# Four attention-and-FFN layers on one core: layer-3 keys made inside the adapter loop, layer-0 evictions ahead of the exponentials, straight attention programs

## The chip, the cores and the metric

One core of a Trainium2 chip. The metric is the device time of one execution in microseconds (us). The engines are named as in the profile: PE (TensorE, matmuls and transposes), PEld (its weight loads), DVE (VectorE), ACT (ScalarE), POOL (GpSimd) and SP (SyncE, which issues DMAs).

## What is computed

Sixteen sequences of 64 tokens with 512 channels go through four layers. Every layer adds an attention over a second input `ctx` and then a feed-forward part (FFN), both on a layer norm of x:

```python
x = x + _L2_xattn_ref(_layernorm(x), ctx_4096, mask, bias, Wq, Wk, Wv, Wo)      # layers 0, 2, 3: 32 heads of 128
x = x + _L2_ffn_ref(_layernorm(x), W_base, b_base, W_gate, W_thr, b_thr, A_w, B_w)
# FFN of layer 2:
w = w / wsum                                  # gate of 8 experts, thresholded
moe = jnp.einsum('ner,ne,eor->no', h, w, B_w) * SCALING
return base + moe.reshape(base.shape)
# attention of layer 3: 4 key/value heads, keys over context and latents
hidden_states = jnp.concatenate([context, latents], axis=1)
k = (hidden_states @ Wk); v = (hidden_states @ Wv)
```

## The kernel before

The program is a chain of blocks: setup, `a0` (attention of layer 0), `f0`, `x1`, `f1`, `a2`, `f2` (adapter FFN of layer 2), `a3`, `f3`. Tokens stand in eight tiles of 128. Every engine has its own in-order program, and semaphores tie them together. fp32 products are made as three fp16 matmuls of high and low halves (`mm3`, L85 to L87), so most values pass ACT (which writes the high half from PSUM) and DVE (which writes the rest as low half) before PE can use them. Weights come as slabs of 128x2048 that are turned to two fp16 halves the same way: a sum of squares on ACT (L434), the total on PE and DVE, a scale on POOL, the high half on ACT (L439) and the low half on DVE (L846).

**Attention.** `Attention.events(t)` lists the work of one period of 8 slots, the same list for all engines, each of which takes its own part of every event. A period covers one projection group; units of heads go through scores, turn, mix and out, one slot apart each. Periods 0 to 8 run in order; ACT, DVE, POOL and SP write periods 1 to 6 once as a hardware loop (`periods`, `Fori(0, 3)` over two periods), PE writes all of them out (`straight`). Period 8 has no projections: it drains the last units and does the first steps of the FFN that follows (`f_stat` statistics on DVE, `f_norm`, `f_turn` transposes on PE, `f_keep` ACT copies, `f_logit`, `f_main`).

In `a0` a query tile (128x512) is evicted by three ACT instructions, two for the squares of the norm (L536, L537) and the high half (L545), and two DVE ones (L947, L952); PE's `q_read` and the projection that follows wait for L952. ACT's list of a slot is: high half of the probabilities (`split_hi`, L579), slab squares (L434), four exponentials (L566), then the tile.

**f2 and layer 3's first steps.** `AdapterFFN` does per tile t: `base(t)` (L2125, four fp32 matmuls 128x512 into a PSUM bank; banks are reused every `deep` = 3 tiles, so base(t+3) waits for the x-add of tile t), a transpose of the gated tile `hw` (L2138), an ACT copy of it to `ht` (L1991), the adapter matmul `main(t)` (L2147) and the DVE x-add (L2094). Into the same loop are woven a3's slabs (`squares_ahead`, `total_ahead`, `high_ahead`, `low_ahead`), the halves of ctx (`ctx_high` L452, `ctx_low` L874), and the norm and transposes of x (`act_step`, `dve_step`, `pe_step`; PE's is L650). When all of it is done, 32 key and value tiles follow (`kv`), 12 matmuls each, alternating over two banks. SP issues the k and v slabs and ctx (2 MB) at the start of f2.

## Time and profile before

| | us |
|---|---|
| median of 3 runs | 2186.36 (2185.17 to 2188.26) |
| the profiled execution | 2187.63 |
| its span in the profile | 2185.8 |
| PE busy | 2057.9 (94% of the span) |
| DVE / ACT / POOL busy | 1343.3 / 1178.4 / 555.0 |
| mean granted TensorE clock | 0.977 |

The profile is taken from one execution. 1.8 us of that execution's time lie outside the span. PE is the busiest engine, so the views to read are those of PE's idle time and of the clock that it was granted. A row of the timeline gives start, length, engine, line, operation, output and input; a bracket behind it tells how long the engine was idle before and what ended that.

### The profile page before, as it was taken

To read this page: it belongs to the slowest core of one execution; us is meant where nothing else is said; L and a number is where in the kernel's file an instruction comes from. 1 tells how busy PE (TensorE), PEld (TensorE's weight loads), DVE (VectorE), ACT (ScalarE), POOL (GpSimd) and SP (SyncE) were. 2 spreads that over 40 slices of the span, in tenths; PEclk is the share of its full clock that TensorE was granted. 3 is DMA by queue.
4 is the path that set the end of the run, shared out by engine and by line. 5 is a ranking of instruction groups with operands and counts; after the bars stand their busy time and mean duration, and the time that the engine had idled before them with its cause. 6 is when DMAs were issued, how large, how long until landed. Compare 5 with 4: busy or idle time off the path is not lost.

```text
span 2185.8 us, 39604 instructions
## 1 busy us (share of the span) xinstructions
PE 2057.9 (94%) x13732; PEld 1131.0 (52%) x13732; DVE 1343.3 (61%) x2722; ACT 1178.4 (54%) x3031; POOL 555.0 (25%) x958
## 2 busy tenths in 40 slices
PE   6799999999879899999999999998889899999998
PEld 3566556656534345555555555555334455555564
DVE  6677776776763756656656656656542466666664
ACT  6677766766432455555555555533222576666651
POOL 4233233233241322122122122113200222222221
PEclk9899999999998999999999999999979999999999
DMA  3222122121002123232232232211200233333211
GB/s 131 61 67 62 45 66 60 47 81 35 27 10 119 61 78 76 71 92 76 71 92 76 72 92 76 51 35 44 113 20 1 63 78 78 82 78 82 59 49 39
DMA packets 181336, 142.92 MB, mean 65 GB/s; under 512 B 158139, under 2 KB 166587, under 8 KB 171283
## 3 DMA queue, kind: packets, MB, share of 16 engines
q1 hardware_dynamic: 180690, 140.37, 23.1%
q8 instruction: 110, 1.80, 0.3%
q14 instruction: 88, 0.71, 0.1%
q10 hardware_dynamic: 448, 0.03, 0.0%
HBM read 100.26 MB, written 2.10 MB: 47 GB/s over the span
## 4 chain that ended last, share of the span: by engine, by line
PE 66%; DVE 13%; ACT 11%; issue 6%; POOL 3%; DMA 0%; DVEq 0%; ACTq 0%; POOLq 0%; SPq 0%
PE bank L85 20%; PE bank L86 20%; PE bank L87 20%; ACT m_E L566 3%; PE bank L2125 3%; DVE m_Sm L1001 1%; ACT m_arena L545 1%; DVE m_x L1052 1%; ACT m_arena L434 1%; ACT m_arena L537 1%; DVE m_A L1046 1%; DVE m_nmax L1018 1%; ACT m_arena L536 1%; DVE m_arena L947 1%; DVE m_arena L846 1%
## 5 line engine op out<-in xcount | busy, mean ns | idle before, releaser
L947 DVE TENSOR_TENSOR m_arena<-bank,m_arena 128x512 f16<-128x512 f32 x320 | 221.1, 691 | 452.9 <-ACT m_arena L545 451.5
L85 PE MATMUL bank<-m_input_parts,m_arena 128*128 128x512 f16 x1120 | 431.0, 385 | 24.8 <-DVE m_arena L952 12.2
L86 PE MATMUL bank<-m_input_parts,m_arena 128*128 128x512 f16 x1120 | 430.2, 384 | 0.0
L87 PE MATMUL bank<-m_input_parts,m_arena 128*128 128x512 f16 x1120 | 429.9, 384 | 0.0
L1064 POOL TENSOR_TENSOR m_E<-m_E,m_rinv 128x512 f32<-128x512 f32 (+1 forms) x192 | 172.2, 897 | 815.0 <-DVE m_rinv L1032 815.0
L566 ACT ACTIVATE m_E<-m_Sm,m_nmax 128x64 f32<-128x64 f32 (+1 forms) x512 | 185.2, 362 | 254.3 <-DVE m_nmax L1022 149.0
L545 ACT ACTIVATE m_arena<-bank 128x512 f16<-128x512 f32 x320 | 189.1, 591 | 232.5 <-PE bank L87 232.3
L85 PE MATMUL bank<-m_wo_t,m_A 128*128 128x512 f16 x768 | 292.4, 381 | 0.0
L86 PE MATMUL bank<-m_wo_t,m_A 128*128 128x512 f16 x768 | 292.2, 381 | 0.0
L87 PE MATMUL bank<-m_wo_t,m_A 128*128 128x512 f16 x768 | 292.0, 380 | 0.0
L1052 DVE SCALAR_TENSOR_TENSOR m_x<-bank,m_osc,m_x 128x512 f32<-128x512 f32 x192 | 143.2, 746 | 79.1 <-PE bank L87 75.5
L85 PE MATMUL bank<-m_arena,m_input_parts 128*128 128x128 f16 (+1 forms) x768 | 186.6, 274 | 2.4 <-DVE m_arena L952 1.6
L85 PEld LDWEIGHTS bank<-m_input_parts,m_arena 128*128 128x128 f16 x1120 | 110.4, 99 | 151.2 <-DVE m_arena L952 14.3
L86 PE MATMUL bank<-m_arena,m_input_parts 128*128 128x128 f16 (+1 forms) x768 | 186.7, 274 | 0.0
L87 PE MATMUL bank<-m_arena,m_input_parts 128*128 128x128 f16 (+1 forms) x768 | 186.7, 274 | 0.0
L87 PEld LDWEIGHTS bank<-m_input_parts,m_arena 128*128 128x128 f16 x1120 | 110.4, 99 | 136.4 <-issue 7.0
L86 PEld LDWEIGHTS bank<-m_input_parts,m_arena 128*128 128x128 f16 x1120 | 110.5, 99 | 116.7 <-issue 6.2
L579 ACT ACTIVATE m_split<-m_E 128x512 f16<-128x512 f32 (+1 forms) x174 | 97.1, 558 | 121.6 <-POOL m_E L1064 117.3
L1061 POOL TENSOR_TENSOR m_w_scale<-m_w_tot,m_consts 128x1 f32<-128x1 f32 x84 | 46.6, 554 | 454.6 <-DVE m_w_tot L840 435.7
L562 ACT ACTIVATE m_E<-bank,m_nmax,m_qk 128x128 f32<-128x128 f32 x256 | 113.5, 452 | 67.4 <-DVE m_nmax L989 67.4
L1046 DVE TENSOR_TENSOR m_A<-bank,m_A 128x512 f16<-128x512 f32 x192 | 130.2, 678 | 6.0 <-ACT m_A L585 5.1
L846 DVE SCALAR_TENSOR_TENSOR m_arena<-m_raw,m_w_scale,m_arena 128x2048 f16<-128x2048 f32 (+1 forms) x58 | 118.0, 2034 | 15.4 <-ACT m_arena L439 13.5
(308 smaller groups left out, 4154.5 us busy)
## 6 DMA issues: line engine op xcount, KB each, us to landing
m_raw<-a_q SPq DMA_DIRECT2D x24, 1024.0 KB, 5.0
m_raw<-a_o SPq DMA_DIRECT2D x24, 1024.0 KB, 5.0
m_raw<-a_k SPq DMA_DIRECT2D x9, 1024.0 KB, 4.9
m_raw<-a_v SPq DMA_DIRECT2D x9, 1024.0 KB, 5.3
m_bias_in<-bias SPq DMA_DIRECT2D x64, 128.0 KB, 2.1
m_arena<-f_w SPq DMA_DIRECT2D x3, 1024.0 KB, 7.6
...
```

The costliest lines, as they stand in the source:

```text
L85: pe.matmul(out, lhs[0], rhs[0], start=first, stop=False)
L86: pe.matmul(out, lhs[0], rhs[1], start=False, stop=False)
L87: return pe.matmul(out, lhs[1], rhs[0], start=False, stop=last)
L545: act.activation(self.dest(name, part, 0), self.shaped(name, src), ACT.Copy).then_inc(s["proj_hi"].sem, 1)
L562: ins = act.activation(k.E[:, b % 2, cols], bank[2 + b % 2][:, cols], ACT.Exp, bias=k.nmax2[:, b % 2, h:h + 1], scale=qk, accum_out=k.rsum ...
L566: ins = act.activation(k.E[:, b % 2, cols], k.Sm[:, b % 2, cols], ACT.Exp, bias=k.nmax[:, b % 2, h:h + 1], accum_out=k.rsum[:, b % 2, h:h ...
L579: act.activation(self.split_dst(b, 0), k.E[:, b % 2, 0:self.keys * HG], ACT.Copy)\
L846: dve.scalar_tensor_tensor(out=self.slab(kind, par, 1), in0=self.raw(j, kind), scalar=self.k.w_scale[:, j % 2:j % 2 + 1], in1=self.slab(ki ...
L947: ins = dve.tensor_tensor(self.dest(name, part, 1), self.shaped(name, bank[m % 2][:, :]), self.dest(name, part, 0), ALU.subtract)
L1046: dve.tensor_tensor(self.mix_dst(b, 1), self.mix_src(), self.mix_dst(b, 0), ALU.subtract).then_inc(s["mixed_lo"].sem, 1)
L1052: dve.scalar_tensor_tensor(out=k.x[:, pair, :], in0=bank[6][:, :], scalar=k.osc[:, g:g + 1], in1=k.x[:, pair, :], op0=ALU.mult, op1=ALU.ad ...
L1064: pool.tensor_tensor(out, a, b, op).then_inc(sem.sem, 1)
```

## The change

- **a0, slots 0 and 4 of periods 1 to 7** (`pair`): ACT does the slab squares ahead of the high half of the probabilities, and the first query tile's three evictions ahead of the four exponentials. PE and DVE keep the tile where it was.
- **Straight programs**: ACT, DVE and POOL write all nine periods of all three attentions out; SP keeps its loop.
- **Layer 3's preparation begins in a2's last period**: SP loads both slabs in period 7, ctx in two halves in period 8; the joint scale, all of ctx's halves and the first slab (keys) are converted between the steps of period 8. `ctx_in` lies in the arena, and the turned tiles of f2 in other free pieces.
- **The adapter loop of f2 and f3**: the eight transposes of `hw` go to two banks, four each, and two 128x512 ACT copies take them back into `hw`. Main(t) is followed by base(t+3). In f2, steps 4 to 11 make two of the 16 key tiles each, in banks 5 and 6; the 16 value tiles stay behind the loop.

```diff
+            pair = self.layer == 0 and slot in (0, 4) and not opening
+            sooner = squared is not None and (pair or self.layer == 3)
+            if sooner and pair:
+                out.append(("w_squares", squared))
             if self.by_dma(t, b - 1):
                 out.append(("split_hi", b - 1))
+            if sooner and not pair:
+                out.append(("w_squares", squared))
+            if pair and todo:
+                out.append(("act_tile", todo[0], slot // 4))
...
-                out.append(("tile", todo.pop(0), slot // 4))
+                out.append(("tile_act_sooner" if pair else "tile", todo.pop(0), slot // 4))
...
+            if t == 8 and self.layer == 2:
+                out += {0: [("n_joint",)], 2: [("n_ctx", 0)], 3: [("n_ctx", 1), ("n_squares",)], 4: [("n_sum",), ("n_ctx", 2)],
+                        5: [("n_ctx", 3)], 6: [("n_convert",)]}.get(slot, [])
...
+    def load_slabs(self, sp):
+        for j in range(2):
+            self.load(sp, self.pre[j], 0, j, 0)
+    def load_ctx(self, sp, c):
+        sp.dma_start(self.k.ctx_in[:, c:c + 2, :], self.dram["ctx_t"][:, c:c + 2, :]).then_inc(self.s["ctx_in"].sem, 16)
...
+                    if t == 7 and slot == 4:
+                        self.next.follower.load_slabs(sp)
+                    elif t == 8 and slot in (0, 2):
+                        sp.wait_ge(*(s["mixed"] if slot else s["scores"]).by(UNITS - 4))
+                        self.next.follower.load_ctx(sp, slot)
...
-        if self.layer == 3 and 3 <= t < 3 + KC:
-            self.ctx_high(act, t - 3)
...
+    def kv_tile(self, n):
+        return (n % 4) * 4 + n // 4 if n < 16 else n
+    def kv_bank(self, n):
+        return self.k.bank[5 + n % 2 if n < 16 else n % 2][:, :]
...
+    def kv_pe(self, pe, n):
+        k, s = self.k, self.s
+        if n == 0:
+            pe.wait_ge(*s["w_lo"].by(1))
+            pe.wait_ge(*s["ctx_lo"].by(KC))
+        if n < 16 and n % 4 == 0:
+            pe.wait_ge(*s["xt_lo"].by(n // 2 + 2))
+        pe.wait_ge(*s["kv_lo"].by(n - 1))
...
+    def keys_of(self, t):
+        return range(2 * (t - 4), 2 * (t - 4) + 2) if 4 <= t < 12 else []
...
-            for m in range(32):
-                act.wait_ge(*s["kv"].by(m + 1))
-                act.activation(k.kv3(m, 0), bank[m % 2][:, :], ACT.Copy).then_inc(s["kv_hi"].sem, 1)
+            for n in range(16, 32):
+                self.kv_act(act, n)
...
-        self.periods(act, emit)
+        self.straight(emit)
...
-        self.periods(dve, emit, ch, self.CHAIN["dve"][self.layer])
+        self.straight(emit)
...
-        self.periods(pool, emit, self.own, self.CHAIN["pool"][self.layer])
+        self.straight(emit)
...
-        for t in range(TILES):
-            if self.follower and t % 2 == 0 and t // 2 < self.follower.NP:
-                self.follower.squares_ahead(act, t // 2)
-            act.wait_ge(*s["ht"].by(t + 1))
-            act.wait_ge(*s["main"].by(t - 1))
-            act.activation(self.ht[:, t % 2, :], self.turn_bank(t), ACT.Copy).then_inc(s["ht_s"].sem, 1)
-            if self.follower and t % 2 and t // 2 < self.follower.NP:
-                self.follower.high_ahead(act, t // 2)
-            if self.follower:
-                self.follower.act_step(act, t)
-        for t in range(TILES, TILES + 2):
-            if self.follower:
-                self.follower.act_step(act, t)
+        for h in range(2):
+            act.wait_ge(*s["ht"].by(h + 1))
+            act.activation(self.hw[:, 4 * h:4 * h + 4, :].rearrange("p t n -> p (t n)"), self.turn_bank(h), ACT.Copy)\
+               .then_inc(s["ht_s"].sem, 1)
+        if self.follower:
+            for t in range(TILES + 5):
+                for n in self.follower.keys_of(t - 1):
+                    self.follower.kv_act(act, n)
+                if t // 2 + 1 < self.follower.NP:
+                    (self.follower.high_ahead if t % 2 else self.follower.squares_ahead)(act, t // 2 + 1)
+                if t < TILES + 2:
+                    self.follower.act_step(act, t)
...
-            if self.follower and t // 2 < self.follower.NP:
-                if t % 2 == 0:
-                    self.follower.total_ahead(dve, t // 2)
-                else:
-                    self.follower.low_ahead(dve, t // 2)
             if self.follower:
-                self.follower.dve_step(dve, t)
-        for t in range(TILES, TILES + 2):
+                self.ahead_dve(dve, t)
             if self.follower:
-                self.follower.dve_step(dve, t)
+                for n in self.follower.keys_of(t):
+                    self.follower.kv_dve(dve, n)
+        if self.follower:
+            for t in range(TILES, TILES + 5):
+                self.ahead_dve(dve, t)
+                for n in self.follower.keys_of(t):
+                    self.follower.kv_dve(dve, n)
+    def ahead_dve(self, dve, t):
+        if t // 2 + 1 < self.follower.NP:
+            (self.follower.low_ahead if t % 2 else self.follower.total_ahead)(dve, t // 2 + 1)
+        if t < TILES + 2:
+            self.follower.dve_step(dve, t)
...
-        turn(0)
-        turn(1)
+        for h in range(2):
+            for t in range(4 * h, 4 * h + 4):
+                pe.wait_ge(*s["hw"].by(t + 1))
+                ins = pe.transpose(self.turn_bank(h)[:, (t % 4) * P:(t % 4 + 1) * P], self.hw[:, t, :], k.ident[:, :])
+            ins.then_inc(s["ht"].sem, 1)
         for t in range(TILES):
-            pe.wait_ge(*s["ht_s"].by(t + 1))
-            pe.matmul(self.main_bank(t), self.ht[:, t % 2, :], self.bm[:, :], start=False, stop=True).then_inc(s["main"].sem, 1)
-            if self.follower and t % 2 == 0 and t // 2 < self.follower.NP:
-                self.follower.sum_ahead(pe, t // 2)
-            if t + 2 < TILES:
-                turn(t + 2)
+            pe.wait_ge(*s["ht_s"].by(t // 4 + 1))
+            pe.matmul(self.main_bank(t), self.hw[:, t, :], self.bm[:, :], start=False, stop=True).then_inc(s["main"].sem, 1)
             if t + self.deep < TILES:
                 self.base(pe, t + self.deep)
             if self.follower:
-                self.follower.pe_step(pe, t)
-        for t in range(TILES, TILES + 2):
-            if self.follower:
-                self.follower.pe_step(pe, t)
+                self.ahead_pe(pe, t)
+        if self.follower:
+            for t in range(TILES, TILES + 4):
+                self.ahead_pe(pe, t)
+    def ahead_pe(self, pe, t):
+        if t % 2 == 0 and t // 2 + 1 < self.follower.NP:
...
+            self.follower.sum_ahead(pe, t // 2 + 1)
+        if t < TILES + 2:
+            self.follower.pe_step(pe, t)
+        for n in self.follower.keys_of(t):
+            self.follower.kv_pe(pe, n)
```

The first place is ACT in a0, slot 4 of a period; what stands there before (`m_split` is the high half of the probabilities, L534/L553 register work):

```order
L585 ACTIVATE m_A<-bank 128x2x4x64 [waits outp,mixed]
L579 ACTIVATE m_split<-m_E 128x256 [waits pt1,probs]
L434 ACTIVATE m_arena,m_w_ss<-m_raw 128x2048 [waits raw1,proj]
L553 REGISTER_ALU
L566 ACTIVATE m_E,m_rsum<-m_Sm,m_nmax 128x64 [waits split_lo,top]
L566 ACTIVATE m_E,m_rsum<-m_Sm,m_nmax 128x64 x3
L533 REGISTER_ALU [waits scores]
L534 REGISTER_ALU [waits a0_q_tot]
L536 ACTIVATE m_arena<-bank 128x8x64 [waits proj]
L537 ACTIVATE m_arena<-bank 128x8x64
L545 ACTIVATE m_arena<-bank 128x8x64 [waits proj]
```

And now, in the changed program (L482 is L434 of before, L668 is L579, L625/L626/L634 are L536/L537/L545, L655 is L566):

```order
L674 ACTIVATE m_A<-bank 128x2x4x64 [waits outp,mixed]
L482 ACTIVATE m_arena,m_w_ss<-m_raw 128x2048 [waits raw1,proj]
L668 ACTIVATE m_split<-m_E 128x256 [waits pt1,probs]
L625 ACTIVATE m_arena<-bank 128x8x64 [waits proj,a0_q_tot,scores]
L626 ACTIVATE m_arena<-bank 128x8x64
L634 ACTIVATE m_arena<-bank 128x8x64 [waits proj]
L655 ACTIVATE m_E,m_rsum<-m_Sm,m_nmax 128x64 [waits split_lo,top]
L655 ACTIVATE m_E,m_rsum<-m_Sm,m_nmax 128x64 x3
```

The squares moved ahead of the wait for the probabilities, and the tile ahead of the exponentials. The second place is DVE at the end of slot 2 of a2's last period; before:

```order
L1046 TENSOR_TENSOR m_A<-bank,m_A 128x512 [waits mixed_hi]
L1052 SCALAR_TENSOR_TENSOR m_x<-bank,m_osc,m_x 128x512 [waits outp]
L1213 BN_STATS m_bn<-m_x 128x6 [waits xadd]
L1215 BN_AGGR m_mv<-m_bn 128x2 [waits f2_dve]
L1217 TENSOR_SCALAR m_var<-m_mv 128x1 [waits f2_dve]
L1011 SCALAR_TENSOR_TENSOR m_Sm<-bank,m_qk,m_bias_in 64x4x64 [waits a2_bias_sum,exped,scores]
```

Now (L1130 is L1052 of before, L953 is `ctx_low`, L1293 is L1213, L1089 is L1011):

```order
L1124 TENSOR_TENSOR m_A<-bank,m_A 128x512 [waits mixed_hi]
L1130 SCALAR_TENSOR_TENSOR m_x<-bank,m_osc,m_x 128x512 [waits outp]
L953 SCALAR_TENSOR_TENSOR m_input_parts<-m_arena,m_joint,m_input_parts 128x16x64 [waits a3_ctx_hi]
L1293 BN_STATS m_bn<-m_x 128x6 [waits xadd]
L1295 BN_AGGR m_mv<-m_bn 128x2 [waits f2_dve]
L1297 TENSOR_SCALAR m_var<-m_mv 128x1 [waits f2_dve]
L1089 SCALAR_TENSOR_TENSOR m_Sm<-bank,m_qk,m_bias_in 64x4x64 [waits a2_bias_sum,exped,scores]
```

A low half of ctx stands between x and its statistics; the same in slots 3, 4 and 5. The third place is PE in the adapter loop, from main(4) on; before:

```order
L2147 MATMUL bank<-m_arena 128x512 [waits f2_ht_s]
L639 MATMUL bank<-m_w_ss,m_ones_b 128x1 [waits w_ss,misc_read]
L2138 MATMUL bank<-m_ident,m_arena 128x128 [waits f2_ht_s,f2_hw]
L2125 MATMUL bank<-m_arena 128x512 [waits x,xt_s]
L2125 MATMUL bank<-m_arena 128x512 x3
L650 MATMUL bank<-m_ident,m_Sm 128x128 [waits xt_lo,xn]
L650 MATMUL bank<-m_ident,m_Sm 128x128 x3
L2147 MATMUL bank<-m_arena 128x512 [waits f2_ht_s]
```

Now (L2243 is L2147, L2221 is L2125, L739 is L650, and L85 to L87 are the first matmuls of key tile 0):

```order
L2243 MATMUL bank<-m_arena 128x512 [waits f2_ht_s]
L2221 MATMUL bank<-m_arena 128x512 [waits x,xt_s]
L2221 MATMUL bank<-m_arena 128x512 x3
L739 MATMUL bank<-m_ident,m_Sm 128x128 [waits xt_lo,xn]
L739 MATMUL bank<-m_ident,m_Sm 128x128 x3
L85 MATMUL bank<-m_input_parts,m_arena 128x512 [waits xt_lo,a3_kv_lo,a3_ctx_lo,w_lo]
L86 MATMUL bank<-m_input_parts,m_arena 128x512
L87 MATMUL bank<-m_input_parts,m_arena 128x512
```

The transpose of `hw` is gone from the loop, and the key matmuls stand in it.

## Rows read from the trace of the kernel before

**Rows 1.** Busy time by stage: stretch, length, busy per engine, granted clock, DMA share, GB/s.
```profile
100.00:500.00 400.00, 389.69 (x3697) 243.18 (x3696) 283.62 (x679) 286.92 (x858) 137.24 (x241) 1.00 0.22 59
800.00:1480.00 680.00, 678.87 (x4198) 349.74 (x4196) 415.56 (x756) 353.18 (x842) 144.80 (x259) 1.00 0.28 74
1485.00:1546.42 61.42, 51.62 (x340) 35.12 (x338) 37.11 (x75) 18.79 (x59) 22.15 (x27) 0.92 0.27 104
...
1552.19:1697.80 145.61, 126.06 (x481) 56.36 (x482) 56.76 (x94) 39.59 (x59) 12.30 (x32) 0.88 0.06 22
1610.73:1697.80 87.07, 85.66 (x384) 38.02 (x385) 22.12 (x32) 19.88 (x33) 0.00 (x0) 0.97 0.00 1
1736.00:2100.00 364.00, 364.00 (x2365) 201.78 (x2363) 230.64 (x419) 243.02 (x655) 84.49 (x147) 1.00 0.31 75
```

**Rows 2.** Waits of 90 to 560 us: us in total, times, longest us.
```profile
PE bank L85 <- DVE m_arena L952: 10.7, 13, 2.1
...
DVE m_Sm L1001 <- issue: 2.6, 2, 1.7
```

**Rows 3.** Timeline of ACT in a0, one slot of these thirteen.
```profile
318.58 0.42 ACT L579 ACTIVATE m_split<-m_E 128x256 f16<-128x256 f32 x1 [1.74 <-POOL m_E L1064]
318.91 1.89 ACT L434 ACTIVATE m_arena<-m_raw 128x2048 bf16<-128x2048 f32 x1
...
322.12 0.57 ACT L536 ACTIVATE m_arena<-bank 128x512 f32<-128x512 f32 x1
```

**Rows 4.** Timeline of PE, the wait of that slot and the longest of the thirteen.
```profile
325.04 0.39 PE L85 MATMUL bank<-m_input_parts,m_arena 128*128 128x512 f16 x1 [0.97 <-DVE m_arena L952]
...
358.71 0.39 PE L85 MATMUL bank<-m_input_parts,m_arena 128*128 128x512 f16 x1 [2.12 <-DVE m_arena L952]
```

**Rows 5.** Busy time by stage, two stretches with a low clock.
```profile
359.00:364.00 5.00, 5.00 (x17) 1.89 (x16) 3.96 (x11) 2.06 (x11) 1.28 (x4) 0.66 0.00 2
...
1591.50:1616.00 24.50, 16.12 (x40) 7.46 (x41) 16.59 (x26) 7.46 (x12) 2.98 (x6) 0.51 0.13 44
```

**Rows 6.** Timeline of DVE in a2's last period.
```profile
1508.64 0.55 DVE L1223 TENSOR_SCALAR m_arena<-m_x,m_mv,m_rstd 128x512 f32<-128x512 f32 x1
...
1512.91 0.69 DVE L1213 BATCH_NORM_STATS2 m_bn<-m_x 128x6 f32<-128x512 f32 x1
...
1515.46 0.98 DVE L1011 SCALAR_TENSOR_TENSOR m_Sm<-bank,m_qk,m_bias_in 64x256 f32<-64x256 f32 x2 [1.45 <-POOL m_bias_in L1064]
...
1523.30 1.48 DVE L1223 TENSOR_SCALAR m_arena<-m_x,m_mv,m_rstd 128x512 f32<-128x512 f32 x1 [0.66 <-POOL m_rstd L1244]
```

**Rows 7.** Timeline of POOL beside the last of these.
```profile
1523.23 1.26 POOL L1318 TENSOR_TENSOR m_x<-m_x,m_arena 128x512 f32<-128x512 f32 x1
```

**Rows 8.** Groups of instructions of 1485 to 1611 us: busy, mean ns.
```profile
L874 DVE SCALAR_TENSOR_TENSOR m_input_parts<-m_arena,m_joint,m_input_parts 128x1024 f16<-128x1024 f32 x4 | 5.1, 1274 | 0.0
...
L846 DVE SCALAR_TENSOR_TENSOR m_arena<-m_raw,m_w_scale,m_arena 128x2048 f16<-128x2048 f32 x2 | 4.7, 2344 | 0.0
```

**Rows 9.** Timeline of PE in the adapter loop.
```profile
1563.09 1.02 PE L2147 MATMUL bank<-m_arena 128*128 128x512 f32 x2
1563.95 0.17 PE L639 MATMUL bank<-m_w_ss,m_ones_b 128*128 128x1 bf16 x1
...
1564.98 3.67 PE L2125 MATMUL bank<-m_arena 128*128 128x512 f32 x8 [0.70 <-DVE m_x L2094]
1568.49 0.60 PE L650 MATMUL bank<-m_ident,m_Sm 128*128 128x128 f32 x4
...
1579.83 2.07 PE L2147 MATMUL bank<-m_arena 128*128 128x512 f32 x2 [3.78 <-ACT m_arena L1991]
```

**Rows 10.** Waits of 1552 to 1611 us.
```profile
PE bank L2147 <- ACT m_arena L1991: 10.3, 5, 3.8
```

**Rows 11.** Timeline of DVE at the start of f2: the gated tiles.
```profile
1551.12 1.70 DVE L2088 TENSOR_TENSOR m_arena<-m_arena 128x128 f32<-128x128 f32 x8
```

**Rows 12.** Waits of the whole program, with no releaser in the profile.
```profile
DVE m_Sm L1011 <- issue: 5.0, 2, 2.6
```

131 lines of the change are left out of this document (85 added, 46 removed).

## The prediction

> **What bounds the kernel now.** I read the busy time by stage first. PE is busy for 364.00 of 364.00 us in the middle of layer 3's attention and for 678.87 of 680 in layer 2's [rows 1]: there the time is the count of matmuls, and no edit of another engine's program can shorten it. PE stands still in three other places. In a0 it is busy 389.69 of 400 us. In a2's last period it is busy 51.62 of 61.42 us. From the first adapter matmul to the end of the value tiles it is busy 126.06 of 145.61 us, at a granted clock of 0.88 [rows 1]. The change touches these three and leaves PE's work as it is, but for some transposes. So each part is worth the idle time, and the half-clock time, that it takes from PE there.
>
> The profiled execution took 2187.63 us, and the median is 1.27 below it. The sum is made against 2187.63, and the 1.27 come off at the end.
>
> **a0.** The waits name what PE stood for: 10.7 us in 13 gaps at its projection matmul, for DVE's L952 [rows 2]. One slot shows the chain. ACT sits idle 1.74 us for the probabilities, then does their high half, 1.89 us of slab squares from 318.91, the exponentials, and only at 322.12 the first of the tile's three evictions [rows 3]; PE gets its operand at 325.04 after 0.97 us of idling, and in the worst slot after 2.12 [rows 4]. The squares need only a slab that lies there, so ahead of the wait they take its 1.74 us. The tile goes ahead of exponentials that last from 320.80 (318.91 + 1.89) to 322.12, 1.3 us. The tile is then ready about 3 us sooner, more than the longest gap. What comes later for it? The exponentials, by the tile's 322.12 to about 323.6, 1.5 us, less the 1.7 that the squares no longer cost them: nothing net. The next thing queued behind them, the high half of the next probabilities, waits for POOL anyway. One of the 13 gaps (0.26) is in the opening period, which the change leaves alone, so 10.7 − 0.3 = **−10.4**. One more thing hangs on the longest gap: right behind it PE ran at a mean clock of 0.66 over 5 us [rows 5], about 3.4 us at the lower level of 1.2 GHz, which costs half of that, **−1.7**. Sum −12.1. Bounds: if half of the gaps close and another wait shows up in the others, −5; with all of it and the smaller waits beside it, −14. I take the upper part, as the margin of 3 us stands against gaps of 0.25 to 2.12.
>
> **Straight programs.** Their price is more code; their gain is that the jump at a loop's end goes. Such jumps show as DVE waits with no releaser: 2.6 us in two in a0 [rows 2], 5.0 in two in a2 [rows 12]. PE has no idle time in a2, so there they are covered and worth **0**; in a0 they lie inside the gaps just counted. If the cover is gone they cost 1.7 to 2.6 us each. That the longer programs stall for their own fetch is a rival below.
>
> The Trainium skill (Runtime: NRT & Kernel Launch, Instruction fetch mechanics) says that a taken branch to a page that isn't loaded stalls, while straight code is fetched ahead and mostly hidden. The waits of [rows 2, 12] agree with its first half; by its second half the straight programs cost nothing, which is what the sum has; were it wrong for programs of this length, the fetch rival below would be the case.
>
> **a2's last period.** Here work is added, some 5.1 us of ctx's low halves and 2.35 of a slab's low half on DVE [rows 8], and the like on ACT and POOL. ACT mostly waits in this period, so its part hides, except where it delays a copy that PE wants. DVE's part stands between x and its statistics. In slot 2 it is on the path: statistics at 1512.91 lead over POOL's rstd and the mask bias to the scores at 1515.46 [rows 6], so a low half of 1.27 us comes on top in full: +1.3. In slots 3 to 5 PE's own 12 out-matmuls of some 2.6 us (at the 0.216 worked out below) cover a part of each; I take 0.6 of 1.27 for each, +1.9 in all. In slot 6 the slab's low half of 2.35 stands ahead of the last tile's statistics; there some 0.3 are slack: +2.1. Sum **+5.3**. Bounds: 0, if everything hides, and 4 × 1.27 + 2.35 + 1 for ACT's part = +8.5. All added DMAs (two slabs and ctx, 4 MB) are issued 10 us or more ahead of their first reader, on an SP queue that has nothing else urgent, and read by engines that wait until then anyway: 0. If ctx came late, its first reader would hold up all of DVE in slot 2.
>
> On this place a rule of the Trainium skill bears. The row: a norm of 128x512 takes 0.55 us alone but 1.48 when POOL's L1318 runs beside it [rows 6, 7]. The Trainium skill (SBUF — State Buffer, SBUF: two separate sides) says that VectorE and GpSimd share one port pair as an exclusive lock, so that one of them blocks for the other's whole instruction. The low halves read two tiles from SBUF and would meet L1318 in slots 2 and 3; by the rule that is 0.3 each, +5.9 in place of +5.3. The sum goes without it.
>
> **The adapter loop.** First its start. Before, main(0) could go when the first transpose had been copied. Now all eight transposes stand ahead of it, so it waits for the last gated tile, which DVE ends at 1551.12 + 1.70 = 1552.82 [rows 11]. Main(0) then comes at about 1553.15 in place of 1552.19: **+1.0**.
>
> Then the loop to the end of the values, 145.61 us before, with the 1.42 at its end that stay [rows 1]. What PE has to do at full clock: eight mains of 0.86 (1563.09 to 1563.95), five bases of 3.51 (1564.98 to 1568.49) and eight turns of 0.44 (three quarters of the 0.60 of their row are seen apart, the rest overlaps) [rows 9], and 32 tiles of 12 matmuls. The latter took 85.66 us for 384 [rows 1]; the first 5.3 us of it are the end of the half-clock stretch [rows 5], in which 12 are done, so one is (85.66 − 5.3) / 372 = 0.216. Sum 6.9 + 17.6 + 3.5 + 0.3 for small ones + 384 × 0.216 = 82.9, in all 111.2. What remains to wait: five bases each wait for the x-add of the main before them. Before, 0.70 us were seen behind a transpose of 0.3 [rows 9], so now some 1.1 each, 5.7 in all; and 1.8 more where DVE is busy with a slab's low half (2.35) in steps 1 and 3. Together 118.7. From step 4 on each step has two key tiles, 5.2 us of PE work, and DVE's and ACT's share of a step is about 4.3 us or less, so PE is the bound: the 10.3 us that main waited for ACT's small copies [rows 10], with 3.78 the longest [rows 9], are gone, and with them, I expect, the half clock: over 24.5 us from 1591.5 it was 0.51 [rows 5], in a stretch in which PE was busy 16.12 us only. 145.61 − 1.42 = 144.2, so **−25.5**. Bounds: −14 if the clock stays low as it did, −27 if the added waits vanish.
>
> **f3** has the same new start (+0.65) and saves about 0.11 on three bases: **+0.3**. **Clock**: longer idle stretches in a2's last period, whose clock is 0.92 already [rows 1], can bring another fall of 3.4 us; I count one, **+1.7** (0 to +3.4).
>
> **Sum**: −12.1 + 5.3 + 1.0 − 25.5 + 0.3 + 1.7 = −29.3, so 2158.3 for the profiled execution and **2157** for the median. Chance 0.55 for this case, by which I mean 2153 to 2162.
>
> **Rivals.**
> - *The clock stays halved in the loop.* PE fell to 1.2 GHz at 1592 and stayed there for some 24 us [rows 5]. If the idling of the first steps (waits of 1.1 to 2 us each) brings such a stretch, the key tiles run at half speed for 20 us and lose 10: **2167**. For it: it happened in this very loop. Against: from 1552 to 1563 PE idled as much, and the two falls in it came after longer waits. Chance 0.16.
> - *a0's gain goes elsewhere.* The tile is early, but PE then waits in another slot for scores or probabilities, now pushed by the tile on ACT. Then a0 gives 5 in place of 12: **2164**. For it: the exponentials' readers are a chain over POOL. Against: they end no later than before. Chance 0.12.
> - *The tail costs little.* If the added conversions hide (ACT is idle for most of the period) and no new fall comes, 5 to 6 us less: **2151**. Chance 0.11.
> - *Slower: instruction fetch.* The straight programs of ACT and DVE are some 40% longer in instructions. Were they to stall as at the loops' ends, 1.7 us each [rows 2], PE would have to see more than 29 / 1.7 = 17 such stalls before the gain is gone; with 20 of them, **2192**. Against it: PE's program is straight already, is by far the longest, and shows 364.00 of 364.00 us busy [rows 1]. Chance 0.04.
> - *It doesn't do what it says.* If the key tiles stay blocked until the loop's end (through the two banks that the transposes of `hw` also use, or a late low half of ctx), PE idles as before there and only half of the 25 is won: **2169**. Chance 0.02.
>
> **Range.** 2147 to 2168 leaves out some 2 in 10: a part of the first and the last rivals, and what lies below. A measurement of this kernel can tell about 0.2%, 4.4 us. Faster by more than that 0.94, within it 0.02, slower 0.04; all but the fetch rival lie far below 2182.
>
> **What the next profile would show.** a0: the wait of PE for L952's successor falls from 10.7 to under 1, PE busy in over 398 of 400 us, no stretch at a clock of 0.66. Last period of a2: PE's idle time grows from 9.8 to some 15 us, spread over slots 2 to 7, with DVE named. Loop: 119 us or so from main(0) to the last value matmul, clock near 1.0, and waits for x-adds of 1 to 2 us in the first five steps alone. I would be wrong if ACT turned up as what PE waits for in steps 4 to 11, if a long half-clock stretch lay there, or if waits with no releaser stood all over ACT's and DVE's rows.

## The result

The changed kernel takes 2151.10 us (median of 3 runs, 2149.67 to 2152.86) where the kernel before takes 2186.36. The ratio is 0.9838 (95% interval 0.9816 to 0.9860): 35 us, or 1.6%, faster. The forecast was 2157, with a range of 2147 to 2168. It held, and the kernel is 6 us faster than the likeliest case. Run again beside other kernels, it took 2152.88 (2149.55 to 2153.63), ratio 0.9836. One execution of a kernel below, the one with the late low halves, took 2690.0 us at a granted clock of 0.75, and it is left out of that kernel's numbers.

The page of its profiled execution (2149.67 us) begins:

```profile
span 2147.9 us, 38029 instructions
...
PE 2040.1 (95%) x13732; PEld 1125.9 (52%) x13732; DVE 1336.4 (62%) x2722; ACT 1175.9 (55%) x3019; POOL 557.6 (26%) x958
```

PE has as many matmul records as before and is busy 17.8 us less. A fall of the busy time is no fall of the work. Where 1.2 GHz is granted, the same matmul is busy for twice as long (in the kernel before, the records of the base matmuls, L2125, follow one another after 0.85 us at 1586 us and after 0.43 at 1566), and the last matmul before a pause is shown as busy for longer than it holds up a stream (below).

To compare stages I cut both programs at records that both have: DVE's adds into x. Counting those of the three attentions, the 1st and the 57th bound the stretch called a0 below, its seven full periods; the 65th is the first of a2; the 121st is the first of a2's last period; the first add of f2 starts the adapter loop; the 129th is the first of a3. The stretch from the 121st to f2's first is called the tail. Busy time by stage in the changed kernel (stretch, length, busy of PE, PEld, DVE, ACT, POOL, granted clock, DMA share, GB/s):

```profile
88.77:532.11 443.34, 441.40 (x4245) 277.61 (x4242) 322.75 (x782) 325.26 (x976) 153.11 (x261) 1.00 0.21 58
532.11:807.04 274.93, 241.70 (x1197) 122.30 (x1196) 167.01 (x340) 111.05 (x230) 82.00 (x116) 0.95 0.17 60
1463.31:1541.14 77.83, 61.71 (x367) 38.51 (x365) 49.67 (x106) 28.73 (x72) 24.50 (x31) 0.91 0.20 68
1541.14:1698.00 156.86, 141.37 (x650) 65.99 (x651) 66.35 (x113) 52.82 (x97) 20.31 (x46) 0.99 0.09 26
```

| stage | before | changed | difference | forecast |
|---|---|---|---|---|
| start to a0's first x-add | 89.09 | 88.77 | -0.3 | 0 |
| a0 | 460.16 | 443.34 | -16.8 | -12.1 |
| a0's last period, f0, x1, f1, a2's start ("the stage behind a0") | 277.63 | 274.93 | -2.7 | 0 |
| a2, seven periods | 656.26 | 656.26 | 0 | 0 |
| the tail: a2's last period to f2's first x-add | 70.22 | 77.83 | +7.6 | +5.3 +1.0 +1.7 |
| f2's loop and the values, to a3's 129th x-add | 182.93 | 156.86 | -26.1 | -25.5 |
| from there through f3, to the last x-add | 446.39 | 446.71 | +0.3 | +0.3 |

So the forecast stands in five stages within 0.6 us, and misses in two: a0, by 4.7, and the stage behind a0, which the change touches by the straight programs alone, by 2.7. The waits of PE in a0 answer to [rows 2]. Of the thirteen behind L952 (now L1030) none is left:

```profile
PE bank L85 <- DVE m_arena L1041: 1.0, 1, 1.0
PE bank L85 <- issue: 0.8, 1, 0.8
```

ACT in one slot of the new order, which answers to [rows 3]. The tile's first eviction starts 2.69 us behind the start of L674; before, it started 5.87 us behind the start of the same instruction (L585 at 316.25, L536 at 322.12), so it comes 3.2 us sooner:

```profile
308.92 0.60 ACT L674 ACTIVATE m_A<-bank 128x512 f16<-128x512 f32 x1
309.42 1.90 ACT L482 ACTIVATE m_arena<-m_raw 128x2048 bf16<-128x2048 f32 x1
...
311.31 0.40 ACT L668 ACTIVATE m_split<-m_E 128x256 f16<-128x256 f32 x1
311.61 0.58 ACT L625 ACTIVATE m_arena<-bank 128x512 f32<-128x512 f32 x1
...
313.17 0.35 ACT L655 ACTIVATE m_E<-m_Sm,m_nmax 128x64 f32<-128x64 f32 x1
```

From 100 to 500 us PE is now busy 399.03 of 400 us, where 389.69 were read before [rows 1] and over 398 were forecast.

PE in the adapter loop, which answers to [rows 9]. L2243 is main, L2221 base, L739 a turn:

```profile
1540.51 0.59 PE L2243 MATMUL bank<-m_arena 128*128 128x512 f32 x1
1541.98 3.67 PE L2221 MATMUL bank<-m_arena,m_wo_t 128*128 128x512 f32 x8 [0.87 <-DVE m_x L2184]
1545.48 0.17 PE L728 MATMUL bank<-m_w_ss,m_ones_b 128*128 128x1 bf16 x1
1545.51 1.10 PE L2243 MATMUL bank<-m_arena 128*128 128x512 f32 x2
```

And its waits up to 1610 us, which answer to [rows 10]:

```profile
PE bank L2221 <- DVE m_x L2184: 6.1, 5, 1.7
```

The 10.3 us for ACT's small copies are gone. What stands in their place is what was foreseen, five waits for x-adds, 6.1 us where 7.5 were assumed. From main(0) to the last value matmul:

```profile
1539.98:1658.11 118.13, 112.04 (x475) 51.35 (x474) 47.94 (x83) 31.45 (x46) 12.80 (x28) 1.00 0.05 18
```

118.13 us were measured where 118.7 were forecast, and 112.04 of PE work where 111.2 were.

### The profile page after: what moved, and what is told of

Its sections match the earlier page's. It is cut to its first block, busy times and chain, and to the rows that moved or that the text cites. A ratio compares the mean times of both kernels' runs of the same rounds, so it can differ in the third digit from the quotient of the medians.

```text
span 2147.9 us, 38029 instructions
## 1 busy us (share of the span) xinstructions
PE 2040.1 (95%) x13732; PEld 1125.9 (52%) x13732; DVE 1336.4 (62%) x2722; ACT 1175.9 (55%) x3019; POOL 557.6 (26%) x958
## 4 chain that ended last, share of the span: by engine, by line
PE 81%; DVE 9%; ACT 5%; issue 3%; POOL 1%; DMA 0%; ACTq 0%; SPq 0%; DVEq 0%; POOLq 0%
PE bank L85 25%; PE bank L86 25%; PE bank L87 25%; PE bank L2221 2%; ACT m_E L655 1%; DVE m_bn L1293 1%; PE bank L1981 1%; ACT m_E L651 1%; DVE m_x L1130 1%; ACT m_arena L487 1%; DVE m_arena L925 1%; DVE m_wo_t L925 1%; PE bank L2243 1%; DMA m_raw<-a_q 0%; PE bank L825 0%
## 5 line engine op out<-in xcount | busy, mean ns | idle before, releaser
L85 PE MATMUL bank<-m_input_parts,m_arena 128*128 128x512 f16 x1120 | 428.4, 383 | 12.6 <-ACT m_input_parts L1779 3.7
L87 PE MATMUL bank<-m_input_parts,m_arena 128*128 128x512 f16 x1120 | 427.6, 382 | 0.0
L634 ACT ACTIVATE m_arena<-bank 128x512 f16<-128x512 f32 x320 | 189.3, 592 | 238.6 <-PE bank L87 238.2
L655 ACT ACTIVATE m_E<-m_Sm,m_nmax 128x64 f32<-128x64 f32 (+1 forms) x512 | 185.4, 364 | 240.2 <-DVE m_nmax L1100 148.5
L85 PE MATMUL bank<-m_wo_t,m_A 128*128 128x512 f16 x768 | 292.6, 381 | 0.0
L87 PE MATMUL bank<-m_wo_t,m_A 128*128 128x512 f16 x768 | 292.4, 381 | 0.0
L1130 DVE SCALAR_TENSOR_TENSOR m_x<-bank,m_osc,m_x 128x512 f32<-128x512 f32 x192 | 143.2, 746 | 78.9 <-PE bank L87 76.7
L85 PE MATMUL bank<-m_arena,m_input_parts 128*128 128x128 f16 (+1 forms) x768 | 186.6, 274 | 2.4 <-DVE m_arena L1030 1.6
L87 PE MATMUL bank<-m_arena,m_input_parts 128*128 128x128 f16 (+1 forms) x768 | 186.7, 274 | 0.0
L87 PEld LDWEIGHTS bank<-m_input_parts,m_arena 128*128 128x128 f16 x1120 | 110.3, 98 | 134.7 <-issue 4.7
L85 PEld LDWEIGHTS bank<-m_input_parts,m_arena 128*128 128x128 f16 x1120 | 110.2, 98 | 133.4 <-issue 5.8
L1139 POOL TENSOR_TENSOR m_w_scale<-m_w_tot,m_consts 128x1 f32<-128x1 f32 x84 | 47.6, 566 | 459.4 <-DVE m_w_tot L919 441.3
L668 ACT ACTIVATE m_split<-m_E 128x512 f16<-128x512 f32 (+1 forms) x174 | 97.0, 558 | 85.2 <-POOL m_E L1142 85.2
L925 DVE SCALAR_TENSOR_TENSOR m_arena<-m_raw,m_w_scale,m_arena 128x2048 f16<-128x2048 f32 (+1 forms) x58 | 117.4, 2024 | 13.8 <-ACT m_arena L487 13.1
```

The costliest lines, as they stand in the source:

```text
L85: pe.matmul(out, lhs[0], rhs[0], start=first, stop=False)
L87: return pe.matmul(out, lhs[1], rhs[0], start=False, stop=last)
L634: act.activation(self.dest(name, part, 0), self.shaped(name, src), ACT.Copy).then_inc(s["proj_hi"].sem, 1)
L655: ins = act.activation(k.E[:, b % 2, cols], k.Sm[:, b % 2, cols], ACT.Exp, bias=k.nmax[:, b % 2, h:h + 1], accum_out=k.rsum[:, b % 2, h:h ...
L668: act.activation(self.split_dst(b, 0), k.E[:, b % 2, 0:self.keys * HG], ACT.Copy)\
L925: dve.scalar_tensor_tensor(out=self.slab(kind, par, 1), in0=self.raw(j, kind), scalar=self.k.w_scale[:, j % 2:j % 2 + 1], in1=self.slab(ki ...
```

## Experiments

Each kernel is the changed one, or the one before, with the edit that is shown.

### a0: the order undone, and the order alone

```diff
-            pair = self.layer == 0 and slot in (0, 4) and not opening
-            sooner = squared is not None and (pair or self.layer == 3)
+            pair = False
+            sooner = squared is not None and ((self.layer == 0 and slot in (0, 4) and not opening) or self.layer == 3)
```

> The changed kernel with a0's ACT order as before (squares behind the probabilities' high half, tile behind the exponentials); all else stays. Theory 1: a0 gave 16.8 us between the first and the 57th x-add, because each of the 13 gaps cost PE more than the idle that the row shows (some 0.2 us each: the last matmul before a gap is shown with 0.38 us, while in a stream the next follows after 0.216), and because the straight programs took the two loop-end stalls. Then undoing the order alone gives back 16.8 less what the loop ends had: 0.75 + 1.57 us of gap and the 1.7 us of half clock behind the longest, so +12.8: about 2164. Rival: what exceeds the predicted 12.1 comes from the straight programs alone; then the order is worth 10.4 less 2.3 = 8.1, about 2159. In the trace: gaps of 0.54 and 0.97 us at PE's projection matmul, and neither 1.30 nor 2.12.

Measured: 2167.86 us (2167.34 to 2168.34), ratio to before 0.9914 (0.9896 to 0.9932). Its a0:

```profile
90.22:546.47 456.25, 444.02 (x4245) 277.77 (x4242) 326.18 (x782) 325.37 (x975) 154.26 (x261) 1.00 0.21 57
```

a0 takes 12.9 us longer than in the changed kernel, where +12.8 was expected. Between the two profiled executions the whole is 18.2 us longer; of the other 5.3, 1.5 lie in the start and 3.6 in the stage behind a0, which vary from run to run (below). Against before, which had the loops, a0 is 3.9 shorter: that is what straight programs give by themselves, the two long gaps and the half clock behind one of them (expected: 0.75 + 1.57 + 1.7 = 4.0).

The other way round, the kernel before with the new order in a0 and its hardware loops kept:

> The kernel before with a0's new ACT order alone, hardware loops kept. Theory 1 (the order alone closes all gaps, the loop-end stalls of 1.7 us lie inside the 3 us by which the tile is early, and each gap cost 0.2 more than its idle): -16.8, about 2169.6. Rival (the straight programs are needed for the two loop-end gaps and the half clock behind one): -12.8, about 2173.6, with PE gaps at the loop ends.

Measured: 2171.80 us (2165.12 to 2172.80), ratio 0.9924 (0.9900 to 0.9947). Its a0:

```profile
89.55:532.89 443.34, 441.40 (x4245) 277.64 (x4242) 322.96 (x781) 325.41 (x976) 152.91 (x261) 1.00 0.22 58
```

443.34 us, the same to the hundredth as with straight programs. The order alone brings all 16.8. The median lies halfway between the two expected values, since the other stages differ by 1 to 3 us from run to run; the stage decides. Theory 1 stands: the two edits overlap, and the lead of the tile covers the loops' ends.

### The hardware loops kept

```diff
-        self.straight(emit)
+        self.periods(act, emit)
```

and so for DVE and POOL.

> The changed kernel with the hardware loops of ACT, DVE and POOL as before; all else stays. Theory 1 (the loop ends stall DVE and ACT 1 to 2.6 us, but the tile is some 3 us early in a0 and PE is covered in a2 and a3): no change that can be told, 2151 within 3 us, with waits without a releaser back in DVE's and ACT's rows and no PE gap behind them. Rival (the straight programs are what made a0 gain more than forecast): 2 to 5 us slower, with PE gaps at the two loop ends near 220 and 345 us.

Measured: 2153.95 us (2153.39 to 2154.87), ratio 0.9852 (0.9834 to 0.9869), against 0.9838 and 0.9836 for the changed kernel: no difference that can be told. The stalls at the loops' ends are back in the waits of the whole program, in a2 where PE has no idle time:

```profile
DVE m_Sm L1089 <- issue: 5.0, 2, 2.5
ACT m_split L668 <- issue: 4.4, 2, 2.3
```

a0 takes 443.35 us. In the changed kernel these two rows are absent; of waits without a releaser, one of 0.2 us on DVE in a0 is left, none in a2 and none on ACT. So the fetch rival is out as well: the straight programs, some 50% (ACT) and 30% (DVE) longer in instructions, stall no more, and they bring nothing either, once the order in a0 is as it is.

### a0: only the squares, only the tile

```diff
-            if pair and todo:
-                out.append(("act_tile", todo[0], slot // 4))
```

with `("tile", ...)` in its old place for all engines.

> The changed kernel, but in a0 only the slab squares go ahead of the probabilities' high half; the tile stays behind the exponentials. Theory 1 (the gaps close by whatever lead the tile gets): the squares fill ACT's 1.7 us of idling, so exponentials and tile come some 1.9 sooner, more than the gaps of 0.54 and 0.97 that straight programs leave; a0's stage from the first to the 57th x-add stays at 443.3 us. Rival (the tile must stand ahead of the exponentials, since what follows them pushes back): some of the 12.9 us that a0 loses without the new order come back, 447 us or more.

Measured: 2159.91 us in one run. Its a0:

```profile
88.79:541.38 452.59, 443.80 (x4245) 277.76 (x4241) 325.95 (x781) 325.36 (x976) 154.26 (x261) 1.00 0.21 57
```

The expectation failed: 9.3 of the 12.9 us come back. ACT's timeline says why:

```profile
313.25 1.90 ACT L480 ACTIVATE m_arena<-m_raw 128x2048 bf16<-128x2048 f32 x1
...
315.14 0.41 ACT L666 ACTIVATE m_split<-m_E 128x256 f16<-128x256 f32 x1
317.00 0.35 ACT L653 ACTIVATE m_E<-m_Sm,m_nmax 128x64 f32<-128x64 f32 x1 [1.45 <-DVE m_nmax L1094]
...
318.34 0.57 ACT L623 ACTIVATE m_arena<-bank 128x512 f32<-128x512 f32 x1
```

The squares went into the 1.74 us of idling, and a new idle time of 1.45 opened ahead of the exponentials, which wait for DVE's maximum. The tile behind them came 0.3 us sooner, and the gaps of 0.97 and 0.56 became 0.68 and 0.26. On this run theory 2 was formed. With only the tile moved (squares behind it):

> The changed kernel, but in a0 only the tile goes ahead of the exponentials; the squares stay behind the probabilities' high half, now behind the tile. Theory 2 (formed on the run with the squares alone, whose gaps fell by 0.28 us only: the exponentials wait for DVE's maximum, so squares moved ahead of them bring the tile little; it is the tile's own move into that time that counts): PE's gaps at the tile stay away and a0's stage is 443.3 us, as with both moves, unless the exponentials, which now start 1.9 us later behind the squares, come back as gaps elsewhere, up to 14 x 0.5 us = 7. Rival (both moves are needed): 447 to 452 us.

Measured: 2164.65 us in one run. Its a0, and PE's waits in it:

```profile
89.69:546.16 456.47, 446.11 (x4244) 276.00 (x4241) 328.84 (x781) 322.50 (x975) 154.34 (x261) 1.00 0.21 57
```
```profile
PE bank L85 <- DVE m_arena L1028: 5.1, 11, 0.5
PE bank L85 <- DVE m_arena L1039: 1.8, 1, 1.8
PE bank L726 <- ACT m_arena L480: 1.2, 1, 1.2
```

456.47 us: nothing is gained over 456.25 with neither. The squares, 1.9 us long, now stand between the tile and the exponentials, everything behind them comes later, and other tiles are late by 0.46. So theory 2 falls too. The stage lies above both what the theory (443.3, at most 7 more) and what the rival (447 to 452) allowed. Neither move is worth much by itself (3.7 and -0.2 us, each from one run's stage); together they are worth 12.9. The squares fill the wait for the probabilities, the tile fills the wait for the maximum that this opens.

### The key tiles behind the loop

```diff
-        return range(2 * (t - 4), 2 * (t - 4) + 2) if 4 <= t < 12 else []
+        return []
...
-            for n in range(16, 32):
+            for n in range(32):
```

> The changed kernel with no key tile in the adapter loop: all 32 tiles follow it, in the same order and banks. Theory 1 (the gain of the loop is key work put where PE waited for the x chain of DVE and ACT): from step 4 on PE has 1.3 us per step against some 3.7 of DVE, six such steps leave some 14 us idle, and the clock falls for a time as before (+3 to +10): 2168 to 2176. Rival (the gain is that of the two transposed banks, since before, PE waited 10.3 us for the small ACT copies): +3 to +5, 2154 to 2156.

Measured: 2164.21 us (2160.89 to 2166.37), ratio 0.9900 (0.9883 to 0.9918): 13.1 us slower than the changed kernel, 11.3 beside its repeat. Between the two theories. The stage, and PE in the loop's last steps:

```profile
1541.46:1709.15 167.69, 147.03 (x649) 67.24 (x650) 66.66 (x113) 53.05 (x97) 20.32 (x46) 0.95 0.08 24
```
```profile
1574.41 0.66 PE L739 MATMUL bank<-m_ident,m_Sm 128*128 128x128 f32 x4 [1.46 <-DVE m_Sm L938]
...
1577.21 0.66 PE L739 MATMUL bank<-m_ident,m_Sm 128*128 128x128 f32 x4 [1.28 <-DVE m_Sm L938]
1580.02 2.37 PE L739 MATMUL bank<-m_ident,m_Sm 128*128 128x128 f32 x8 [2.15 <-DVE m_Sm L938]
```

The stage is 10.8 us longer. Without keys PE idles 5.2 us more (4.9 of it in three waits for DVE's norm) and has 5.7 us more of busy time for the same work, at a clock of 0.95 in place of 0.99. I had expected 14 us of idling. From the last base (1566.68) to the first key matmul (1583.80) PE had 17.1 us, less than the 22 that six steps of 3.7 us would take: the last x-adds of DVE start at 1572.07, 1574.87 and 1577.67, so its step is 2.8 us and not 3.7.

### The two banks alone

In the kernel before, the transposes go to two banks and two copies take them back; nothing else is changed.

```diff
-            act.activation(self.ht[:, t % 2, :], self.turn_bank(t), ACT.Copy).then_inc(s["ht_s"].sem, 1)
...
+        for h in range(2):
+            act.wait_ge(*s["ht"].by(h + 1))
+            act.activation(self.hw[:, 4 * h:4 * h + 4, :].rearrange("p t n -> p (t n)"), self.turn_bank(h), ACT.Copy)\
+               .then_inc(s["ht_s"].sem, 1)
```

> The kernel before, with the eight transposes of the gated tile in two banks and two ACT copies back into it ahead of the loop, and nothing else changed. Theory 1 (in the loop before, PE waited 10.3 us for small ACT copies that stood behind slab and ctx work in ACT's queue, and the clock fell behind the longest of these waits): they go, the start comes 1.0 later, some of the idling moves to the turns; -8 to -14, 2172 to 2178. Rival (without key tiles PE waits for the turns instead, as long as before): within 3 us of 2186.

Measured: 2182.88 us (2177.16 to 2186.18), ratio 0.9984 (0.9972 to 0.9997), 3 us. That is at the edge of what the rival allowed and far from the 8 to 14 us of the theory: the rival is right. PE's waits in the loop, to be read against [rows 10]:

```profile
PE bank L650 <- DVE m_Sm L859: 10.5, 4, 5.3
...
PE bank L639 <- ACT m_arena L434: 4.5, 2, 2.8
PE bank L2126 <- DVE m_x L2095: 3.0, 3, 1.2
```

The 10.3 us behind ACT's copies did not go, they moved: to the turns behind DVE's norm and to the slab sums behind ACT's squares. The stage takes 178.39 us. With it the 26 us of the loop can be laid out, in the one order in which the parts were added: 182.93 before, 178.39 with the banks (-4.5), 167.69 when slab and ctx work have moved to a2's last period too (-10.7, for which that period pays 7.6 less the later start), 156.86 with the keys in the loop (-10.8). The move to a2's last period was not run without the banks.

### a2's last period: where the added work goes

First, the next tile's statistics ahead of the added low halves:

```diff
-            if t == 8 and self.layer == 2:
-                out += {0: [("n_joint",)], 2: [("n_ctx", 0)], 3: [("n_ctx", 1), ("n_squares",)], ...
             if t == 8 and slot < 7:
                 out.append(("f_stat", slot + 1))
+            if t == 8 and self.layer == 2:
+                out += {0: [("n_joint",)], 2: [("n_ctx", 0)], 3: [("n_ctx", 1), ("n_squares",)], ...
```

> The changed kernel, but in a2's last period DVE does the statistics of the next tile ahead of ctx's and the slab's low half, and so on all engines in that place. Theory 1 (the low halves stood on the path x-add, statistics, rstd, bias, scores): slot 2 gives back 1.4 us, which now lie in DVE's 1.45 us wait for the bias, slot 3 and slots 4 to 6 about 0.6 each; -3.4, about 2147.7. Rival (PE or ACT set the pace of this period, the low halves ride along): within 1 us of 2151.

Measured: 2155.22 us (2154.36 to 2155.72), ratio 0.9863 (0.9846 to 0.9879). The tail takes 78.4 us, as in the changed kernel (77.8; 78.3 in its repeat). The gain failed to come, and not for the rival's reason. DVE, then POOL, in slot 2:

```profile
1498.15 0.15 DVE L1297 TENSOR_SCALAR m_var<-m_mv 128x1 f32<-128x1 f32 x1
1498.22 1.27 DVE L953 SCALAR_TENSOR_TENSOR m_input_parts<-m_arena,m_joint,m_input_parts 128x1024 f16<-128x1024 f32 x1
1500.73 0.98 DVE L1089 SCALAR_TENSOR_TENSOR m_Sm<-bank,m_qk,m_bias_in 64x256 f32<-64x256 f32 x2 [1.23 <-POOL m_bias_in L1142]
```
```profile
1498.38 1.52 POOL L1328 TENSOR_TENSOR m_rstd<-m_var,m_consts 128x1 f32<-128x1 f32 x1 [0.90 <-DVE m_var L1297]
1499.88 0.72 POOL L1142 TENSOR_TENSOR m_bias_in<-m_bias_in,m_mask 128x256 f32<-128x256 f32 x1
```

DVE started the low half in its idle time, but the POOL instruction that this idle time waits for, 128x1 elements, took 1.52 us beside it in place of 0.55. Of the 1.27 us that were to be hidden 0.97 came back as POOL's. It is no chance of one slot. Five of POOL's eight rstd instructions began beside a low half in this run; they took 1.52, 1.52, 1.58, 1.52 and 2.61 us, and each ended 0.41 us behind DVE's instruction, the last one beside the slab's low half of 2.35:

```profile
1527.73 2.35 DVE L925 SCALAR_TENSOR_TENSOR m_arena<-m_raw,m_w_scale,m_arena 128x2048 f16<-128x2048 f32 x1
```
```profile
1527.88 2.61 POOL L1328 TENSOR_TENSOR m_rstd<-m_var,m_consts 128x1 f32<-128x1 f32 x1 [2.15 <-DVE m_var L1297]
```

The other three took 0.55. In the changed kernel low half and rstd stood apart, and all eight took 0.55; another 128x1 instruction of POOL, the slab's scale (L1139 at 1512.14), stood beside the third low half there and took 1.52.

So in the second version only two low halves stay in the slots, and the rest goes where DVE waits for the last logits:

```diff
+            if t == 8 and self.layer == 2:
+                out += {2: [("n_low", 0)], 3: [("n_low", 1)], 7: [("n_low", 2), ("n_low", 3), ("n_wlow",)]}.get(slot, [])
```

with ACT's high halves in their slots and its squares in slot 2.

> The changed kernel, but in a2's last period only two low halves of ctx stay (each behind the statistics of its slot); the other two and the slab's low half go to the end of slot 7, where DVE waits 5.5 us for the last logits (they take 4.9), and the slab's squares go to slot 2, where ACT waits 5.6 us. Theory 1: the tail loses all but some 1 us of the 6.7 that it grew by, -5.5, about 2145.6, with the same loop behind it. Rival (the conversions are not what lengthened the tail, or they push the gates in their new place): within 2 us of 2151. The clock's falls in the tail can shift either by 2 to 3 us.

Measured: 2147.61 us, the median of three (2143.36 to 2149.18), ratio 0.9817 (0.9795 to 0.9840). The tail takes 71.69 us, 6.1 less than in the changed kernel, about as expected. By the medians the whole gained 3.5 us, and the intervals overlap; the two profiled executions differ by 0.5 only, since the start was 1.6, the stage behind a0 2.9 and the loop 0.9 longer this time. In the third version the squares and one high half of ctx go to the start of slots 2 and 3 and one low half behind the norm of slot 3:

> The changed kernel, with every added conversion of a2's last period put into an idle stretch that its trace shows: the slab's squares at the start of slot 2 and the second high half of ctx at the start of slot 3 (ACT waits 5.4 us there for the maximum), its low half behind the norm in slot 3 (DVE waits 1.25), the first low half behind the statistics, two low halves and the slab's at the end of slot 7 (5.5 us). Theory: the tail from the last looped x-add to f2's first takes 70.5 us or so, as before the change (70.2), against 71.7 with only the lows late and 77.8 in the changed kernel; in all 5 to 7 us faster than the changed kernel run beside it, if the clock falls alike. Rival (ACT's high halves in slots 4 to 6 or the late lows still lengthen it): 72 us or more.

Measured: 2145.40 us (2143.36 to 2149.03), ratio 0.9807 (0.9793 to 0.9821), beside the changed kernel itself on the same chip with 2152.88, ratio 0.9836 (0.9823 to 0.9850): 7.5 us faster, and the intervals don't meet. The tail:

```profile
1466.36:1538.58 72.22, 60.56 (x367) 39.91 (x365) 50.83 (x106) 28.96 (x72) 25.49 (x31) 0.93 0.21 74
```

72.22 us, where 70.5 was expected and 72 or more was the rival's mark, so by the tail the rival is right, though the whole gained 7.5 where the theory said 5 to 7. I had left out two things of my own: f2's start, 0.9 us later by its transposes, and POOL's 0.97 in slot 2, since one low half still stands beside its rstd. By the tail alone this version is no better than the second (71.69); of the 7.3 us between its profile and that of the changed kernel's repeat, 6.1 lie in the tail, 1.3 in the stage behind a0 and 1.3 in the loop, less 1.5 for a longer start. The late low halves are not free either: in both versions they meet POOL's 128x512 instruction into x (L1413, L1417), and one of them takes 2.3 us in place of 1.27, POOL's 2.2 in place of 1.27. Which of the two versions is faster stays open.

### The changed kernel again

> The changed kernel itself, beside the others on one chip. Theory on the clock: the stage from a0's end to a2's ninth x-add takes either 274.9 us with 27.3 us at half clock or some 277.7 with 34.1, by whether a0's 57th x-add falls before or after 532.4 us from the span's start (532.11 and 532.39 gave the one, 532.52 and later the other). Rival: the shorter stage belongs to the changed program and comes in every profile of it.

Measured: 2152.88 us. Its first two stages:

```profile
89.12:532.46 443.34, 441.40 (x4245) 277.54 (x4242) 322.69 (x781) 325.25 (x976) 153.11 (x261) 1.00 0.21 58
532.46:809.97 277.51, 243.41 (x1197) 123.60 (x1196) 167.10 (x341) 111.16 (x230) 82.00 (x116) 0.94 0.17 59
```

The same program took 2.6 us longer in the stage behind a0 than in its first profile, at a clock of 0.94 in place of 0.95. The expectation put the border at 532.4 us, and the profile fell on the side that it named (its "a2's ninth x-add" is the 65th of all, a2's first). The rival, that the shorter stage belongs to the changed program, is out. Over the profiles whose a0 takes 443.3 us:

| a0's end | 532.11 | 532.39 | 532.46 | 532.52 | 532.89 | 532.90 | 533.75 | 533.93 |
|---|---|---|---|---|---|---|---|---|
| stage behind it | 274.9 | 275.0 | 277.5 | 277.5 | 277.8 | 277.7 | 277.9 | 276.2 |

The order of PE's work in that stage is the same in all of them; those with 532.89 and 532.90 keep the hardware loops. The last value shows that it is no matter of two levels alone. And the time at which a0 ends can't be all of it: with the squares alone (541.38) and the tile alone (546.16) the stage takes 275.9 us, with the order undone (546.47) 278.6. In the first profile 27.3 us of the stage ran at 1.2 GHz, in the repeat 34.1. What decides between them was not found; one test that came out on the right side of a border drawn through four values does not show that it is the time.

## Why the prediction was right, and where it was not

**The whole.** The median undercuts the 2157 by 5.9 us. 4.7 of them are a0's; the start, the tail and the loop bring the rest (0.3, 0.4 and 0.6). The range held, but a0 alone lies outside the bounds that were put on it (-5 to -14).

**What bounds the kernel** was read rightly: a2's seven periods give nothing (656.26 us in both kernels) and a3 gives nothing, and the three places with idle PE gave all of the change.

**a0, -12.1 forecast, -16.8 measured.** What was wrong is the size of the term 10.7 - 0.3 = -10.4, and the reasoning behind it had a hole. *The size:* the idle time fell from 460.16 - 446.20 = 13.96 us to 443.34 - 441.40 = 1.94, by 12.0 where 10.4 were put down: the gap of the opening period (0.26) closed too, one wait for L963 (now L1041) fell from 1.92 to 0.97, and one of 0.22 for the slab squares went. These make 1.4 of the 1.6 us by which the idle time fell further than forecast. PE's busy time fell as well, by 4.8 us for the same 4245 matmuls. The half clock behind the longest gap is 1.7 of it, as forecast. The other 3.1, over the 14 gaps that closed, are 0.2 each: a matmul of 512 columns is shown with 0.38 us, while the next one follows it after 0.216 in a stream, so 0.17 of the time behind it are shown as busy though PE stands. The run with the order undone shows it without any half clock: 2.6 us more of busy time with 13 more gaps. The step "10.7 - 0.3 = -10.4" took the idle time of the rows for the cost of the waits. That the remaining 0.03 to 0.05 per gap has the same cause is argued, not shown. *The reasoning:* "the tile is then ready about 3 us sooner", by the squares' 1.74 and the exponentials' 1.3, held for both moves together (3.2 us in the slot shown above), but I had costed them as if each brought its share. The runs with one of them showed 3.7 and -0.2 us. What I had missed is that the exponentials wait for DVE's maximum, which the rows before hid, since the squares stood in that time.

**Straight programs, 0 forecast:** right, given the order. By themselves they are worth 3.9 us, which the order makes unnecessary. The Trainium skill (Runtime: NRT & Kernel Launch, Instruction fetch mechanics) has straight code fetched ahead, with the cost mostly hidden. The trace agrees: in the changed kernel ACT and DVE show no stall that before did not, at some 1.5 and 1.3 times the length.

**a2's last period, +5.3 and +1.7 for the clock, and +1.0 for f2's start: 8.0 forecast, 7.6 measured.** Right in its sum, for this profile: 3.4 us more of the tail ran at 1.2 GHz than before, which is the 1.7 that was put down; in the repeat it was 6.8 us more, and the tail took 78.3. In slot 2 the low half stood in the path, as said. The slab's low half, too, cost what it was given (from a2's last x-add to the last norm 4.68 us in place of 2.55, +2.1), f2's start less (from that norm to main(0) 13.07 in place of 12.64, +0.4 for +1.0). Three of the four low halves of ctx:

```profile
1492.96 1.47 DVE L953 SCALAR_TENSOR_TENSOR m_input_parts<-m_arena,m_joint,m_input_parts 128x1024 f16<-128x1024 f32 x1
...
1511.98 1.27 DVE L953 SCALAR_TENSOR_TENSOR m_input_parts<-m_arena,m_joint,m_input_parts 128x1024 f16<-128x1024 f32 x1
...
1517.89 1.27 DVE L953 SCALAR_TENSOR_TENSOR m_input_parts<-m_arena,m_joint,m_input_parts 128x1024 f16<-128x1024 f32 x1
```

The first of these rows begins while POOL's L1411 runs (1492.08, 1.27 us), and takes 0.2 us more than the third, which stands alone; the one of slot 3 (1502.86) is like the first. The second began ahead of POOL's L1139 and was not held up. The Trainium skill (SBUF — State Buffer, SBUF: two separate sides) has one engine block for the other's whole instruction, and 0.3 in each of two slots was worked out by that ahead of the run. The trace agrees in kind, not in full: at 1492.96 POOL's instruction had 0.39 us left, and 0.2 were lost. It was left out of the sum. Its larger part I had not seen: the rule works on POOL as well, and the 1.52 us of its 128x1 instruction in the run with the statistics first are what decided there. Slot 2 cost what was put down: against the start of the period, the norms of the first three tiles come as before, and the one behind slot 2 comes 1.25 us later (1.3 forecast). By the last norm it is 7.18 us, but how slots 3 to 5 share what lies between was not tested and can't be read off these two profiles, since their stretches at 1.2 GHz lie in different slots.

**The loop, -25.5 forecast, -26.1 measured.** Right, and by its own steps: 112 us of PE work (111 forecast), waits for five x-adds (6.1 for 7.5), no wait for ACT, a clock of 1.00 up to the last value matmul. The story around it was one-sided: it put the gain down to the waits for ACT's small copies. Alone, the two banks gave 4.5 us in the loop and 3 in all, since DVE's and ACT's slab and ctx work stood behind the copies as the next limit. The gain needs all three parts, and keys in the loop count twice: they fill 5 us of idling and keep the clock up for another 5.7.

**f3, +0.3:** measured +0.65 at the start and -0.33 in the loop.

**Not in the forecast: the stage behind a0, -2.7.** It isn't owed to the change: its granted clock varies between executions of the same program (0.95 and 0.94), and the repeat gave the 2.6 back. What decides it stays open. So of the 38 us between the two profiles some 35 are owed to the change.

**The rivals.** The clock stayed at 1.00 in the loop, so the first is out; a0's gain did not go elsewhere, though with one of its two moves it would have (the tile alone: nothing); the tail cost what was put down; no fetch stalls were seen; the keys ran in the loop (first key matmul at 1570.31, behind base(7)), so the last is out too.
